# A gated cross-attention and FP4 feed-forward block: three ring slots for x, attention values parked in DRAM, hidden activations rounded in place, and another order of the prologue

## The reference

```
q = layernorm(x) @ Wq.T + bq ;  k = ctx @ Wk.T ;  v = ctx @ Wv.T + bv
x = x + tanh(g_xattn) * (softmax(q k.T / sqrt(512)) v @ Wo.T + bo)
y = layernorm(x)
h = silu(Q(y) @ Q(w_gate).T) * (Q(y) @ Q(w_up).T)      # 1408 hidden
x = x + tanh(g_ffn) * (Q(h) @ Q(w_down).T)
```

## Time and profile before

| | |
|---|---|
| median of 3 runs | 833.4 us (832.52 to 834.1) |
| span of the profiled execution | 832.3 us |
| its own time | not listed apart; the median lies 1.1 us above the span |
| PE busy | 822.4 us, 99% of the span, 4102 matmuls |
| DVE busy | 650.7 us (78%) |
| ACT busy | 459.9 us (55%) |
| POOL busy | 400.5 us (48%) |

### The profile page before, as it was taken

One profiled execution on the slowest core, in us unless ns is written; L12 is line 12 of the kernel. 1 busy time (PEld: TensorE's weight loads), 2 busy tenths in 40 slices (PEclk: granted clock), 3 DMA queues, 4 the chain that ended last, 5 costly groups with the idle time before them and its releaser, 6 DMA issues.

```text
span 832.3 us, 11653 instructions
## 1 busy us (share of the span) xinstructions
PE 822.4 (99%) x4102; PEld 417.0 (50%) x4102; DVE 650.7 (78%) x967; ACT 459.9 (55%) x930; POOL 400.5 (48%) x333
## 2 busy tenths in 40 slices
PE   9999999999999999999999999999999999999998
PEld 5555445444554445444544454445544454444445
DVE  5887899898998698877878688778876878776654
ACT  2778675547555666456563755366646565344320
POOL 3498797764334353444333543454444533444421
PEclk9999999999999999999999999999999999999999
DMA  9723703553243434532641255224433443222232
GB/s 318 285 70 103 157 13 97 122 128 92 48 80 106 108 82 89 129 56 54 114 120 40 55 110 136 61 60 99 97 61 61 85 85 73 58 54 55 48 75 73
DMA packets 192817, 78.21 MB, mean 94 GB/s; under 512 B 176387, under 2 KB 178037, under 8 KB 192759
## 3 DMA queue, kind: packets, MB, share of 16 engines
q1 hardware_dynamic: 192759, 77.47, 39.6%
HBM read 22.76 MB, written 8.39 MB: 37 GB/s over the span
## 4 chain that ended last, share of the span: by engine, by line
PE 93%; ACT 3%; DVE 2%; issue 1%; DMA 1%; POOL 1%; POOLq 0%; ACTq 0%; DVEq 0%
PE banks L1918 60%; PE banks L2037 27%; DVE banks L1417 1%; PE banks L2053 1%; PE banks L1912 1%; PE banks L1971 1%; PE banks L1999 1%; PE banks L1998 1%; PE banks L2143 1%; DMA x_T<-x_parts 1%; PE banks L2150 0%; PE banks L2008 0%; PE banks L2160 0%; PE banks L2165 0%; PE banks L2155 0%
## 5 line engine op out<-in xcount | busy, mean ns | idle before, releaser
L1918 PE MATMUL banks<-wgu_hi,x_T 128*128 128x512 f16 (+1 forms) x1536 | 439.3, 361 | 1.6 <-DMA x_T<-x_parts 0.9
L1918 PE MATMUL banks<-wgu_lo,x_T 128*128 128x512 f16 (+1 forms) x768 | 277.5, 361 | 0.0
L1918 PEld LDWEIGHTS banks<-wgu_hi,x_T 128*128 128x128 f16 x1536 | 150.3, 98 | 155.6 <-issue 1.3
L2037 PE MATMUL banks<-wd,arena 128*128 128x512 f16 x1023 | 227.2, 379 | 0.0
L2037 PEld LDWEIGHTS banks<-wd,arena 128*128 128x128 f16 x1023 | 99.7, 98 | 117.4 <-issue 0.6
L648 POOL TENSOR_TENSOR arena<-arena,h_r 128x1024 f32<-128x1024 f32 (+1 forms) x60 | 93.2, 1554 | 115.3 <-DVE h_r L1372 115.3
L648 POOL TENSOR_TENSOR arena<-arena,h_s 128x1024 f32<-128x1024 f32 x64 | 90.7, 1418 | 88.6 <-DVE arena L1419 53.6
L1918 PEld LDWEIGHTS banks<-wgu_lo,x_T 128*128 128x128 f16 x768 | 75.1, 98 | 76.8 <-issue 0.3
L648 POOL TENSOR_TENSOR xwork<-xwork,x_s 128x512 f32<-128x512 f32 x32 | 38.4, 1201 | 152.0 <-DVE xwork L1419 152.0
L1052 ACT ACTIVATE arena<-banks,scal 128x512 f32<-128x512 f32 (+1 forms) x96 | 61.9, 647 | 84.9 <-PE banks L1918 84.8
L1571 DVE SCALAR_TENSOR_TENSOR arena<-arena,scal,banks 128x512 f32<-128x512 f32 (+1 forms) x90 | 62.2, 694 | 56.3 <-PE banks L1918 53.5
(11 more groups left out here) (199 smaller groups left out, 1043.6 us busy)
## 6 DMA issues: line engine op xcount, KB each, us to landing
ring<-in_x_dram SPq DMA_DIRECT2D x8, 1024.0 KB, 5.1
out_dram<-ring SPq DMA_DIRECT2D x31, 256.0 KB, 2.2
arena<-in_L_ffn_w_down_dram SPq DMA_DIRECT2D x4, 704.0 KB, 5.0
arena<-in_L_ffn_w_gate_dram SPq DMA_DIRECT2D x5, 512.0 KB, 9.7
arena<-in_L_ffn_w_up_dram SPq DMA_DIRECT2D x5, 512.0 KB, 9.6
ring<-in_L_xattn_Wk_dram SPq DMA_DIRECT2D x4, 256.0 KB, 6.1
ring<-in_L_xattn_Wq_dram SPq DMA_DIRECT2D x4, 256.0 KB, 6.8
wd<-in_ctx_dram SPq DMA_DIRECT2D x1, 1024.0 KB
```

The costliest lines, as they stand in the source:

```text
L1918: ended = e.matmul(at, l, r, start=(i == 0), stop=(i == len(terms) - 1))
L2037: ended = e.matmul(by_k(down_ps(t)[:, :], KD), l, r, start=(k == 0 and i == 0), stop=(k == KH - 1 and i == 2))
```

## The change

- The ring of x has three slots. A new buffer `late` of three slots holds the weights under way and `valo_raw`; `wo_T` and `gu_sr` move into slots 1 and 2 of the ring. The load of batch 1 now waits also for the product that reads `wo_T` last (`bvwo_mm`).
- `valo` is gone. The five pieces of values are written to a DRAM tensor (`park_values`) and loaded batch by batch into one of two buffers (`load_values`), the loads of batches 1 and 2 in the prologue, each other one at the first tile of its block. In the main list of SP the loads of x batches 2 and 3 change: batch 2 right behind `h_turn(1)`, batch 3 by the store of batch 0.
- `h` is made, divided, rounded and multiplied in place, in one of three buffers; `hidden(t)` waits for `h_low(t-3)`. `h_divide` no longer waits for the step before, and `h_times(0)` no longer for the moved down weights.
- `value_tops` reads the raw values as they stand (128x2048 and 104x512 in two reductions and a maximum) and stands in the prologue, between `down_round(0)` and `down_round(1)`; it was one reduction of 77x3072 behind `x_round(5)`.
- The written lists have another order. On ACT `ln1_stats(1)` goes from ahead of `exps(0)` to behind `prob_copy(0)`, ahead of `gu_low(9)`, `gu_squares(10)` and `gu_high(10)`. On DVE `gu_round(9)` and one `down_tops` go behind `softmax(0)`. The loop from tile 7 on has the same order.

The diff, cut to its core. Left out are removed helpers, the same renamings in other places, and exchanges of neighbours for tiles 1 to 6 and ahead of the stretch that the prediction is about.

```diff
-    SLOTS = 4
+    SLOTS = 3
...
-        valo = sb("valo", [P, NBATCH, D])
...
+        late = sb("late", [P, 3 * SLOT])
+
         def stage(i):
-            return ring[:, i * SLOT:(i + 1) * SLOT].rearrange("p (r n) -> p r n", r=KD)
-
-        stage_a, stage_b, w_T = stage(1), stage(2), stage(3)
-        valo_raw = ring[:, 2 * SLOT:2 * SLOT + CT * D].rearrange("p (r n) -> p r n", r=CT)
-        wo_T = valo[:, 0:KD, :]
+            return late[:, i * SLOT:(i + 1) * SLOT].rearrange("p (r n) -> p r n", r=KD)
+
+        stage_a, stage_b, w_T = stage(0), stage(1), stage(2)
+        valo_raw = late[:, SLOT:SLOT + CT * D].rearrange("p (r n) -> p r n", r=CT)
+        wo_T = ring[:, SLOT:2 * SLOT].rearrange("p (r n) -> p r n", r=KD)
+        v_park = nc.dram_tensor("v_park", [ROWS, D], F32, kind="Internal").ap()
...
-        h_buf = [None, cut(HID)]
-        h_q = cut(HID)
+        h_low_buf = cut(HID)
+        spare = cut(HID)
...
-        h_buf[0] = cut(HID)
-        h_v, h_c = cut(HID), cut(HID // 2).bitcast(BF16)
-        assert CT * D <= 2 * SLOT - HID
-        h_early = {1: ring[:, 4 * SLOT - HID:4 * SLOT], 2: ring[:, 2 * SLOT:2 * SLOT + HID]}
+        h_mid_buf, h_top_buf = cut(HID), cut(HID)
+        h_c = cut(HID // 2).bitcast(BF16)
+        h_early = late[:, 3 * SLOT - HID:3 * SLOT]
+        v_bufs = [arena[:, taken[0] + i * D:taken[0] + (i + 1) * D] for i in range(2)]
+        assert taken[0] + 2 * D <= 2 * KH * D and SLOT + CT * D <= 3 * SLOT - HID
 
         def h_of(t):
-            return h_early[t] if t in h_early else h_buf[t % 2]
+            return (h_mid_buf, h_top_buf, h_early)[t] if t < 3 else (h_low_buf, h_mid_buf, h_top_buf)[t % 3]
+
+        def h_before(t):
+            return {4: 0, 5: 1}.get(t, t - 3)
...
+            both = v_bufs[b % 2].bitcast(F16)
...
+        gu_sr = ring[:, 2 * SLOT:2 * SLOT + 2 * NWB]
...
+            return h_c if r % 2 == 0 else h_early[:, 0:HID // 2].bitcast(BF16)
...
+        v_parked = sem("v_parked")
+        v_loaded = [sem(f"v_loaded{i}") for i in range(2)]
+
+        def values_there(b):
+            return v_loaded[b % 2], 16 * ((b + 1) // 2)
...
-            def move_values(n):
-                for q, o, k, d0 in value_moves(n):
-                    w.wait_ge(val_sb, -(-(n + 1) * KEYS // P))
-                    if n >= KD:
-                        w.wait_ge(gu_q, NPAIR)
-                    e.dma_start(valo[d0:d0 + k, n, :], valo_raw[o:o + k, q, :]).then_inc(loads[f"valo{n}" if n < STACKED else "valo_rest"], 16)
+            def park_values(r):
+                rows = rows_of(r)
+                w.wait_ge(val_sb, r + 1)
+                e.dma_start(v_park[r * P:r * P + rows, :], valo_raw[0:rows, r, :]).then_inc(v_parked, 16)
+
+            def load_values(b):
+                w.wait_ge(v_parked, 16 * CT)
+                w.wait_ge(gu_last, LAST_MOVES)
+                w.wait_ge(d_moved, 32)
+                if b > 2:
+                    w.wait_ge(att_mm, TILES * (b - 1))
+                e.dma_start(v_bufs[b % 2][0:KEYS, :], v_park[b * KEYS:(b + 1) * KEYS, :]).then_inc(v_loaded[b % 2], 16)
...
+            w.wait_ge(bvwo_mm, 1)
             load_x(1)
...
             x_turn(0)
             x_turn(1)
-            move_values(1)
-            move_values(2)
+            park_values(0)
+            move_down(0)
+            park_values(1)
+            park_values(2)
             x_turn(2)
-            move_values(3)
-            move_down(0)
-            move_values(4)
-            move_values(5)
-            move_values(6)
-            move_values(7)
+            park_values(3)
+            park_values(4)
+            load_values(1)
+            load_values(2)
             move_down(1)
             move_down(2)
             move_down(3)
             x_turn(3)
             h_turn(0)
-            w.wait_ge(h_div[1], 2)
-            load_x(3)
             h_turn(1)
+            w.wait_ge(gu_q, NPAIR)
+            load_x(2)
             x_turn(4)
-            w.wait_ge(h_div[1], 3)
-            load_x(2)
             h_turn(2)
             x_turn(5)
             h_turn(3)
             x_turn(6)
             stack_values(2)
+            h_turn(4)
...
 
             def h_divide(t, i):
                 w.wait_ge(h_rec[i], t + 1)
-                if t > 0:
-                    w.wait_ge(h_quant[i], t)
-                w.wait_ge(d_neg, KD)
-                times_blocks(h_v[:, PARTS[i]], h_of(t)[:, PARTS[i]], h_r[:, part_blocks(i)]).then_inc(h_div[i], 1)
+                v = h_of(t)[:, PARTS[i]]
+                times_blocks(v, v, h_r[:, part_blocks(i)]).then_inc(h_div[i], 1)
 
             def h_times(t, i):
-                if t > 0:
-                    w.wait_ge(h_lo[i], t)
-                else:
-                    w.wait_ge(d_moved, DOWN_MOVES)
+                v = h_of(t)[:, PARTS[i]]
                 w.wait_ge(h_rounded[i], t + 1)
                 w.wait_ge(h_scaled[i], t + 1)
-                times_blocks(h_q[:, PARTS[i]], h_v[:, PARTS[i]], h_s[:, part_blocks(i)]).then_inc(h_quant[i], 1)
+                times_blocks(v, v, h_s[:, part_blocks(i)]).then_inc(h_quant[i], 1)
 
...
+                w.wait_ge(d_neg, KD)
+                square(h_c[:, PARTS[i]], h_of(t)[:, PARTS[i]]).then_inc(h_const[i], 1)
...
             key_copy(4)
             ln1_apply(0)
             gu_squares(5)
             gu_high(0)
+            vo_copy(0)
+            gu_squares(6)
             gu_high(1)
...
             gu_high(8)
             gu_high_of(6)
-            gu_squares(9)
-            vo_copy(3)
             xn_copy(0, 3)
-            ln1_stats(1)
+            gu_high_of(7)
             gu_high(9)
-            gu_high_of(7)
-            gu_high_of(8)
             gu_low(8)
             exps(0)
+            key_copy(5)
+            gu_high_of(8)
+            gu_high_of(9)
             prob_copy(0)
+            ln1_stats(1)
             gu_low(9)
             gu_squares(10)
-            gu_high_of(9)
             gu_high(10)
-            key_copy(5)
             x_stats(0)
             key_copy(6)
             x_apply(0)
             x_stats(1)
+            gu_high_of(10)
             key_copy(7)
-            gu_high_of(10)
             x_squares(0)
             key_copy(8)
             x_high(0)
             key_copy(9)
...
             gu_high(11)
-            x_stats(2)
             x_squares(1)
+            down_squares(0)
             gu_low(10)
             gu_low(11)
-            down_squares(0)
+            x_stats(2)
+            gate_silu(0, 0)
             x_apply(2)
-            gate_silu(0, 0)
...
             x_stats(3)
             down_squares(1)
+            ln1_apply(1)
             x_high(1)
+            down_folds()
+            gate_silu(0, 1)
             down_squares(2)
-            down_folds()
-            ln1_apply(1)
-            gate_silu(0, 1)
             xn_copy(1, 0)
...
             def value_tops():
-                w.wait_ge(loads["valo_rest"], 16 * rest_moves())
-                e.tensor_reduce(top_v[0:KEYS, :], valo[0:KEYS, STACKED:NBATCH, :].rearrange("p b n -> p (b n)"), axis=AX_X,
-                                op=ALU.max, apply_absolute_value=True).then_inc(max_made, 1)
+                last = rows_of(CT - 1)
+                w.wait_ge(val_sb, CT)
+                e.tensor_reduce(top_v, valo_raw[:, 0:CT - 1, :].rearrange("p r n -> p (r n)"), axis=AX_X, op=ALU.max, apply_absolute_value=True).then_inc(*step())
+                e.tensor_reduce(rest_v[0:last, :], valo_raw[0:last, CT - 1, :], axis=AX_X, op=ALU.max, apply_absolute_value=True).then_inc(*step())
+                w.wait_ge(dve_step, step.n)
+                e.tensor_tensor(top_v[0:last, :], top_v[0:last, :], rest_v[0:last, :], ALU.max).then_inc(max_made, 1)
 
...
                 if t == 2:
-                    for b in range(1, STACKED):
-                        w.wait_ge(loads[f"valo{b}"], 16 * len(list(value_moves(b))))
-                    w.wait_ge(loads["valo_rest"], 16 * rest_moves())
+                    w.wait_ge(d_neg, KD)
                 if t == 3:
                     w.wait_ge(d_moved, DOWN_MOVES)
                 if t > 3:
-                    w.wait_ge(h_div[1], 1 if t == 4 else t - 1)
+                    w.wait_ge(h_lo[0], h_before(t) + 1)
+                    w.wait_ge(h_lo[1], h_before(t) + 1)
...
             gu_round(7)
-            down_tops(0)
             gu_round(8)
-            gu_round(9)
             value_row()
             softmax(0)
+            gu_round(9)
+            down_tops(1)
             sums(0)
             value_rows(0)
             values(0, 0)
             gu_round(10)
             values(0, 1)
-            down_tops(1)
             x_scales(0)
             values(0, 2)
             x_divide(0)
+            values(0, 3)
             x_round(0)
             down_tops(2)
             down_tops(3)
             down_top_of()
             x_low(0)
             down_scales(0)
-            down_scales(1)
-            values(0, 3)
```

(15 more changed lines are left out.)

179 lines of the change are left out of this document (83 added, 96 removed).

## The result

The changed kernel took 844.95 us (median of four, 843.58 to 846.06), the one before 833.22 (832.52 to 834.1): ratio 1.0141, 95% interval 1.0128 to 1.0153, 11.7 us slower. The forecast was 836.3 us, with a range to 839.8: the sign was right, the size wrong by a factor of four. The profiled execution took 843.58 us, with a span of 841.8, 9.5 above the span before. The traced execution is the fastest of its four, with a mean granted clock of 0.996 (two had spans of 844.1 and 844.3 us at 0.990), while the trace before, 1.8 us under 834.1, fits the slowest of its four: so the traces show 9.5 of the 11.7 us.

A forecast was written before the change was run, and what follows sets the result against it. TensorE was taken as the bound, busy 589.5 of 592.0 us from 240 us on. Span 832.3 + 2.6 (up to tile 1) + 0.3 (tiles 2 and 3) = 835.2, median 1.1 above: 836.3 us, range 832.4 to 839.8.

The forecast's parts named there:

- Step 1: ACT's ln1_stats(1) behind prob_copy(0): TensorE waits 4.1 us for gu_high(10); key_product(7) comes 3.6 us later.
- Step 2: Chain of x behind gu_high(10) on ACT: x_apply(0) +3.4 us, DVE's x_scales(0) goes along.
- Step 3: value_tops in DVE's prologue: 3.1 us ahead of x_low(1), of which 1.5 us fill idle time.
- step 5: Sum up to tile 1: gate_up(1,0,0) +2.6 us by DVE, +2.5 by TensorE; bounds +1.3 and +5.0.
- Step 4: DVE's x_low(1) no longer collides with POOL: 0.7 us instead of 3.08, a gain of 2.4 us.
- Step 6: Tiles 2 and 3: x_low(3) behind h_round(0,1) makes x_turn(3) late, costing 0.3 us against half a us of slack.
- Step 7: Parking, later load_x(1), third ring slot and in-place rounding: nothing, bounds together -0.3 and +1.5 us.
- Worse collisions: Rival: x_low(1) meets a running POOL instruction (+2.4), x_turn(3) 1 us late: 839.4 us, chance 0.17.
- Paid for itself: Rival: TensorE saves 1.2 us early, DVE fills all 2.8 us of idle time: about 834.5 us, chance 0.19.
- faster: Rival: statistics hidden, no new wait at gu_subtract(10), old waits of 2.8 us go: 830.6 us, chance 0.12.
- The loop: Rival: x loads or an h buffer late, 0.5 to 1 us in seven blocks: 840 or more, chance 0.04.

The follow-up runs named there:

- e7: Kernel before with DVE's order of the change from gu_round(7) to value_rows(4), the four down_scales spread apart: 837.03 us, 1.0042.
- e6: Kernel before with value_tops alone moved, in its new form, to between down_round(0) and down_round(1): 836.64 us, 1.0036.
- e4: Changed kernel with DVE's list from x_low(0) to value_rows(2) as before and POOL's x_stats(2) again behind down_divide(1): 844.56 us, 1.0134.
- e14: Kernel before with x_stats(2) alone moved, on ACT behind gu_low(11) and on POOL behind down_divide(3): 835.62 us, 1.0037.
- e15: Changed kernel with x_stats(2) put back as before on both ACT and POOL: 844.14 us.
- e3: Kernel before with ACT's ln1_stats(1) alone moved to behind prob_copy(0): 839.74 us, 1.0081.
- e17: Changed buffers, ln1_stats(1) behind gu_high(11), lists old up to about 145 us, then as changed except value_tops and h_round(0,1): 837.66 us, 1.0047.
- e5: Changed buffers and parking, lists as in the kernel before except ln1_stats(1) behind gu_high(11) and ln1(1) ahead of down_divide(1): 833.63 us, 1.0006.
- e16: Changed kernel with ln1_stats(1) behind gu_high(11) and x_stats(2) as before on ACT and POOL: 839.96 us.
- e1: Changed buffers, parking and new value_tops at its old place, lists of TensorE, ACT, DVE and POOL as in the kernel before: 841.22 us, 1.0091.
- e2: Changed kernel with ACT's ln1_stats(1) behind gu_high(11) and POOL's ln1(1) ahead of down_divide(1): 840.01 us, 1.0079.
- e11: Kernel before with vo_copy(0) behind gu_high(0), gu_round(9) behind softmax(0), values(0,3) behind x_divide(0): 831.52 us, 0.9981.
- e18: Changed buffers, old lists except ln1_stats(1) behind gu_high(11), vo_copy(0) behind gu_high(0), gu_round(9) behind softmax(0), values(0,3) behind x_divide(0): 831.57 us, 0.9978.
- e12: Changed kernel with TensorE's gu_subtract(10) moved behind key_product(7): 845.21 us, 1.0145.

## Why the prediction was right and wrong

**Step 1, right in mechanism and in its wait, a term missing.** The wait was forecast at 4.1 us and is 4.06. The sum left out what follows it: `key_product(7)` took 3.64 us for 2.34. From 88 to 91 us the clock stood at 0.50 to 0.52, the lower of its two levels (1.2 GHz), and behind the wait of 2.59 us it was 0.65 and then 0.50, from 125 to 129 us; the stretches of the earlier trace rows have 1.00 before. Worked out from the shares below 1.00 in the rows, (0.48 + 0.50 + 0.50 + 0.23) and (2 x 0.35 + 2 x 0.50), each fall took 1.7 us of full clock, idle moments included. The matmuls felt 2.3 us of the 3.4: the 154 from `key_product(7)` to `gate_up(1)` took 41.4 us without the idle time, the same 154 before 39.1. The Trainium skill (TensorE: Matmul & The Clock Gate, "HAM oscillation — how this bites in real kernels") says that idle gaps throw the engine back to half rate and that the start after them is paid cold. The trace agrees with these two waits; had the rule been weighed, there would have been a rival with the 4.1 us and more.

**Step 2, right.** `x_apply(0)` +2.4 for +3.4.

**Step 3 and step 5, the steps that failed.** `value_tops` took 2.28 + 0.68 + 0.16 = 3.1 us, as forecast, and DVE's idle time shrank by 0.5 us where 1.5 was forecast. But the DVE stretch up to `x_low(1)` grew by 6.0 us where 3.1 - 1.5 = 1.6 was forecast. The sum takes DVE's other work as unchanged, a term put at nothing without a reason, and that is what failed: the four `down_scales` and `x_scales(1)` had 0.20 + 0.14 + 0.55 + 0.14 + 0.70 = 1.7 us in their first small operations before, and 0.20 + 0.20 + 2.31 + 1.65 + 2.13 = 6.5 after, 4.8 us more. The two passes of `down_round(0)` took 1.0 us less. e7 has nearly the same lengths in the kernel before (2.13, 2.32, 1.89), at +3.9 us. The prediction cited the Trainium skill for `x_low` (SBUF — State Buffer, "Who interferes with whom") and not for what the same list there says of `tensor_scalar`, that it too can take both ports and contend. By that rule each of the three small operations that moved could wait for a 2.59 us multiplication. The trace agrees.

**How that reached TensorE.** Step 5 gave `gate_up(1)` +2.6 by DVE or +2.5 by TensorE; it came at +5.5. It did not wait for its input: `x_turn(1)` was issued at 128.44 and landed 2.7 us later, at 131.2, 1.4 us ahead of the first matmul. TensorE was late by itself. `att_turn(1,0)` began at 125.21 for 119.25 before, +6.0, behind `ln1_apply(1)`, for which the sum of step 5 has no term. (The wait for `key_copy(7)`, put at 0.5 us there, did not arise.) From there to `gate_up(1,0,0)` two old waits (0.69 and 0.93 us) were gone and slow matmuls took 1.2 us more. The clock's first fall was hidden at this point, as far as the order of the rows tells: without it TensorE would have stood longer for `xn`. And `ln1_apply(1)` was late by way of DVE: ACT's `x_squares(1)` waited 5.83 us for `x_divide(1)`, 6.4 us later than before, and with it what stands behind it on ACT.

**Step 4, right.** `x_low(1)` is 0.69 us and the gain of 2.4 us was had, since POOL came to `down_times` only at 128.32. It hangs on that: in e6 the same gain was lost to the operation ahead (3.90 for 1.62); e4 and e7 have 3.07 and 3.08. Whether a collision hits `x_low` or its neighbour depends on POOL's start, and POOL's start on ACT.

**Not in the prediction: `x_stats(2)`.** The diff moves it on two engines, and I counted only those moves that stand on DVE's path. It holds up `x_apply(2)` (2.51 us of waiting), `x_stats(3)`, `down_squares(1)` and `ln1_apply(1)`, which began at 124.27 (118.30 before) and gave TensorE its wait of 2.59 us. Alone it costs 2.5 us (e14); put back in the changed kernel, the wait for `xn` goes (e15).

**Why undoing one part brought so little.** The parts alone cost 6.7 (e3), 3.5 (e6), 3.9 (e7), 2.5 (e14) and 4.0 (e17, against e5), together 20.6, and the whole 11.7. In the changed kernel two things are late to the same place: TensorE itself, with the wait for `xn`, and DVE, which ends `hidden(0,0)` only 0.7 us before `gate_up(0,2,1)` takes its bank and whose `x_turn(1)` lands 1.4 us early. Whoever takes TensorE's lateness away meets DVE's at once. And it grows: with ACT earlier POOL starts earlier and meets `down_round`, 3.9 us for 1.62 (e15, e16; 2.56 and 2.37 in e4), and the longer wait brings the clock down for longer. Undoing ACT's lateness thus made DVE's worse.

**Step 6, mechanism right, size wrong.** `x_low(3)` did wait for `h_round(0,1)`, and `x_turn(3)` was issued 11.2 us later than before, with a wait of 2.34 us for 0.3 forecast. Of the 11.2 us 2.7 are the two operations of `h_round(0,1)` (0.54 + 2.17), as counted; 8.6 were there already at `x_low(2)` (142.08 for 133.51), from step 5. The landing was misread too: 4.5 us for `x_turn(1)` alone, 3.0 to 3.1 for all others before, so that tile 3 had 1.9 us of slack and not 0.5.

**Step 7.** Right for buffers and parking (e5), wrong for the lists behind 145 us, which the prediction left out as exchanges of neighbours: 4.0 us (e17). For `load_x(1)` it was right for the reason it gives, that the reader is later too; had it not been, the price was 8 us (e1).

**The rivals.** "Worse collisions" named the right mechanism at the wrong operations. "Paid for itself" and "faster" fell with e2: even without the wait the order loses. "Faster" is what e11 and e18 make of it with three moves. The loop loses nothing: 592.00 of 592.00 us.

**What stays open.** How the 11.7 us split between the wait of step 1 with its clock, the collisions and `x_stats(2)`: each has a price alone, and they overlap. Which exchanges make the 4.0 us of the late order. And where the two executions at a clock of 0.990 lost the 2.3 us that the traced one did not.

## What to carry to other kernels

Price every step that a reordering moves, on every engine, and also those that stay where they are but now run beside another engine's long operation: small operations of 0.2 us become 2.3. A wait of TensorE can cost more than itself, in e3 5.4 us of waiting and 1.6 of slower matmuls. When two chains are late to the same place, undoing one shows nothing: try parts alone in the kernel before, and from the changed kernel undo whole stretches of all lists.

## What was unexpected of the hardware

- A 128x88 `tensor_scalar` of DVE took 0.14 to 0.20 us by itself and 1.65 to 2.32 beside the whole of POOL's 128x1408 multiplication of 2.59 us; a 128x32 one 2.13. Reductions of 128x1408 took 1.6 us in either case.
- The collision runs both ways: POOL's `rstd`, one number per partition, took 0.54 us before and 2.41 after, beside DVE's two passes of `down_round(0)`, and the last step of `x_stats(2)` 1.23 beside the second.
- After waits of 2.59 and 4.06 us TensorE's clock fell to the lower level; after the wait of 2.34 us at 171 us no fall shows (1.00 in 150 to 240). The length of the wait alone does not decide: in e12 the clock fell behind one of 1.84 us (0.57 from 81 to 85 us), in e2 it stayed at 1.00 behind one of 1.94 us at the same place.
